# A mixture-of-experts kernel: the first layer's bias moves from TensorE to VectorE, two of eight weight splits from VectorE to GpSimd

## The chip, the cores and the metric

One core of one Trainium2 chip runs the program. The metric is the device time of one execution in microseconds (us); lower is better. The core has five engines that run their own instruction queues and meet at semaphores: TensorE (PE, matmuls; PEld is its weight load), VectorE (DVE), ScalarE (ACT), GpSimd (POOL) and SyncE (SP), which here only issues DMAs to 16 shared DMA engines.

## The reference

Three stages work on `x` of 8x64 tokens (512 rows) of width 512: a cross attention over `ctx_1024`, a self attention with given weights, and a mixture of experts. The change is in the third, whose whole computation is

```
gates = softmax(x @ Wg + bg);  top 2 of E=8 experts are kept and renormalised to g
h  = gelu(x @ W1[e] + b1[e])        # W1[e]: 512 x 2048, b1[e]: 2048
eo = h @ W2[e] + b2[e]              # W2[e]: 2048 x 512
x  = x + sum_e g[e] * eo[e]
```

## The kernel before

**Tiles.** Each token goes to two experts, so there are 1024 token rows. The kernel sorts them by expert into `sorted_x` in DRAM, each expert padded to whole tiles of 128 rows. With these inputs there are ten tiles: experts 0 and 1 have two each, experts 2 to 7 one each. I call them tile 0 to tile 9; expert e's last tile is its "change" tile, in which the weights of expert e+1 are brought in. `for_tiles` runs the same loops on every engine, with register bounds.

**Weights.** An expert's W1 and W2 are cut into eight units of 128x2048 fp32 (1 MB each), four of W1 and four of W2, in the order in which a tile uses them (`UNIT_ORDER`: W1 q0, q1, q2, W2 q0, W1 q3, W2 q1, q2, q3). SP loads a unit into one of four ring slots (`wu_raw`). ScalarE rounds it to `wu_hi` (`unit_hi`, L1454), VectorE makes the rest `wu_lo = wu_raw - wu_hi` (`unit_lo`, L1597), and that frees the slot: the load of unit v waits for `wu_lo` of the unit four places earlier (`load_next`, L1311). There is one set of eight `wu_hi`/`wu_lo` buffers, so `unit_hi(v)` for the next expert also waits until TensorE has used unit v of this one. All matmuls are done as three products (hi x hi, hi x lo, lo x hi), 12 of them for each quarter of a layer.

**A tile on TensorE**, in this order: `layer1(0)`, `layer1(1)`, `turn_hidden(0)`, `layer1(2)`, `turn_hidden(1)`, `layer2(0)`, `layer1(3)`, `turn_hidden(2)`, `layer2(1)`, `turn_hidden(3)`, `layer2(2)`, `turn_gathered(t + 1)`, `layer2(3)`. Each `layer1(q)` begins with one more matmul (L1678), ones x `b1rows`, which puts the bias into PSUM; `b1rows` holds the two halves (hi and lo) of the bias in rows 0 and 1 and zeros below. ScalarE's `gelu(q)` (L1460) reads the PSUM bank and writes `hid`; TensorE turns `hid`; `hidden_hi(q)` (ACT, L1466) and `hidden_lo(q)` (DVE, L1602) split it for `layer2(q)`. For the next tile `gathered_hi`/`gathered_lo` (L1440, L1579) split its turned tokens, and `layer1(0)` of the next tile waits for that (`g_lo`), for its weights and for the bias rows (`b1row_in`). At the end of a tile VectorE adds `b2row` and writes `eo` (L1620).

**The order on each engine is written by hand** and is in-order: whatever waits holds up what stands behind it. In a change tile VectorE does hidden_lo(0), unit_lo(0), unit_lo(1), hidden_lo(1), unit_lo(2), unit_lo(3), hidden_lo(2), unit_lo(4), hidden_lo(3), unit_lo(5), gathered_lo, eo, unit_lo(6), unit_lo(7). SP issues: tokens of the next tile (L1327, 256 KB), units 4 to 7 of expert e+1, then, after all four layer1 quarters, the bias rows of e+1 (L1320, 16 KB), units 0 to 3 of e+2, the store of `eo` (L1361, 256 KB) and `b2row` (L1323, one 2 KB row spread over 128 partitions, 256 KB).

**Before the first tile** the biases are split on chip: `b1_raw` is loaded, ScalarE and VectorE make its halves, SP writes them to DRAM (`b1_parts`) and GpSimd clears `b1rows`. Then VectorE makes unit_lo(4) to (7) of expert 0 (`first_lo`, L1499) ahead of its first tile's work. GpSimd scatters the sorted rows before the loop and fetches the results after it; during the tiles it has nothing to do.

Of the kernel before, what the change touches and what calls it, by code (L numbers as in the profile page):

```python
# [22 lines left out]

def perceiver_kernel(nc, x_in, ctx_in, Wq, bq, Wkv, bkv, Wproj, bproj,
# [38 lines left out]
    with ExitStack() as whole:  # L63
# [1149 lines left out]
        b1rows = sb(scope, "b1rows", [P, H], FR)  # L1213
        ones_r = sb(scope, "ones_r", [P, P], FR)
# [84 lines left out]
        with nc.Block() as block:  # L1299

            @block.sync
            def _(sp):
                sp.dma_start(Wg_raw[:, :, :], Wg.rearrange("(k p) e -> p k e", p=P)).then_inc(sem("wg_in"), 16)
                sp.dma_start(bgc[:, :], bg.rearrange("(e o) -> e o", o=1)).then_inc(sem("bg_in"), 16)
                sp.dma_start(b1_raw[:, :], b1.rearrange("e (c p) -> (e c) p", p=P)).then_inc(sem("b1_in"), 16)
# [26 lines left out]
                sp.wait_ge(sem("b1_split"), 1)  # L1332
                for part, b1_part in enumerate((b1_hi, b1_lo)):
                    sp.dma_start(b1_dram[part].rearrange("(r c) -> r c", c=P), f32(b1_part[:, :])) \
                        .then_inc(sem("b1_out"), 16)
                sp.wait_ge(sem("b1_out"), 32)
                sp.wait_ge(sem("b1rows_zeroed"), 1)
# [37 lines left out]
            def _(pool):  # L1375
                nc.gpsimd.memset(f32(b1rows[:, :]), 0.0).then_inc(sem("b1rows_zeroed"), 1)
# [113 lines left out]
            def _(dve):  # L1490
# [6 lines left out]
                def first_lo(v):  # L1497
                    dve.wait_ge(sem("wu_hi_done"), v + 1)
                    nc.vector.tensor_tensor(wu_lo(v), wu_raw[:, v % RING, :, :], f32(wu_hi[:, v, :, :]),  # L1499
                                            ALU.subtract).then_inc(sem("wu_lo_done"), 1)  # L1500

                dve.wait_ge(sem("b1_hi"), 1)
                nc.vector.tensor_tensor(b1_lo[:, :], b1_raw[:, :], f32(b1_hi[:, :]), ALU.subtract) \
                    .then_inc(sem("b1_split"), 1)
# [79 lines left out]
                dve.wait_ge(sem("b1_out"), 32)  # L1584
# [7 lines left out]
                def tile(e, t, change):  # L1592
                    def unit_lo(v):
                        if not change:
                            return
# [38 lines left out]
            def _(pe):  # L1634
# [120 lines left out]
```

## Time and profile before

| what | us |
|---|---|
| median of three runs (1578.81 to 1582.57) | 1578.88 |
| the profiled execution's own time | 1581.12 |
| its span | 1579.4 |
| mixture of experts, first to last tile (1294.5 to 1562.9 in the span) | 268.4 |
| TensorE busy | 1348.1 (85%) |
| VectorE busy | 956.2 (61%) |
| ScalarE busy | 756.9 (48%) |
| GpSimd busy | 45.5 (3%) |

Times inside the profile count from the start of the span. "Busy" of an engine says nothing of what it waited for; the DMA share is the mean over 16 engines of the time in which they had a packet under way, and can be near 1 at less than the highest rate. The profiled execution took 2.2 us longer than the median of the runs.

### The profile page before, as it was taken

The page shows a single profiled execution, that of the slowest core. Times are in us where ns is not written, and L with a number is a line of the kernel's source. Part 1 is how long each engine was busy: PE and PEld are TensorE (multiplying, and loading weights), DVE is VectorE, ACT ScalarE, POOL GpSimd, SP SyncE. Part 2 cuts the span into 40 slices and gives each one's busy share as a digit, 9 for nine tenths or more (in the row PEclk, how much of TensorE's full clock was granted, in tenths as well). Part 3 has the DMA queues.
Part 4 walks back from the last instruction along what each step waited for, and adds up shares of the span by engine and source line. Part 5 has one row for each costly group of instructions (what it writes and reads, how often), then busy time and mean ns, then how long its engine had stood idle before and what let it go on. Part 6 is the DMA issues. An engine that isn't in the chain of part 4 may idle for free. (4 is left out here: it accounts for less than half of the span.)

```text
span 1579.4 us, 21880 instructions
## 1 busy us (share of the span) xinstructions
PE 1348.1 (85%) x7363; PEld 1163.3 (74%) x7364; DVE 956.2 (61%) x1495; ACT 756.9 (48%) x1322; POOL 45.5 (3%) x50
## 2 busy tenths in 40 slices
PE   5999999999999999999999997306979529999995
PEld 4888888888888888888888886204758428777774
DVE  4666666666666666666666665345747564378782
ACT  3455555555555555455455554211222244387771
POOL 0000000000000000000000000021000030000001
PEclk8999999999999999999999999657979769999998
DMA  4210110110110110010110000275225264579993
GB/s 173 78 54 28 31 53 27 30 53 27 30 53 27 30 53 27 28 55 27 27 56 27 26 12 7 60 167 107 54 52 214 85 233 152 188 276 350 334 320 98
DMA packets 129458, 147.18 MB, mean 93 GB/s; under 512 B 66296, under 2 KB 66680, under 8 KB 129408
## 3 DMA queue, kind: packets, MB, share of 16 engines
q1 hardware_dynamic: 128144, 142.54, 28.9%
q0 software_dynamic: 1280, 4.20, 0.8%
q8 instruction: 20, 0.33, 0.1%
q14 instruction: 14, 0.11, 0.0%
HBM read 126.06 MB, written 20.64 MB: 93 GB/s over the span
## 5 line engine op out<-in xcount | busy, mean ns | idle before, releaser
L497 DVE SCALAR_TENSOR_TENSOR Ks<-ps_scores,bkc,Ks 64x384 fp32r<-64x384 f32 (+2 forms) x254 | 160.5, 632 | 205.2 <-ACT Ks L381 202.3
L459 ACT ACTIVATE Pr<-ps_scores,stat 128x705 f32<-128x705 f32 (+1 forms) x128 | 119.1, 931 | 324.3 <-DVE stat L590 324.3
L147 PE MATMUL ps_scores<-cT_hi,Wkv_hi 128*128 128x384 f32 (+2 forms) x508 | 179.7, 354 | 6.4 <-DVE Wkv_lo L519 6.4
L148 PE MATMUL ps_scores<-cT_lo,Wkv_hi 128*128 128x384 f32 (+2 forms) x508 | 176.0, 346 | 0.0
L149 PE MATMUL ps_scores<-cT_hi,Wkv_lo 128*128 128x384 f32 (+2 forms) x508 | 175.9, 346 | 0.0
L147 PE MATMUL ps_scores<-Wkv_hi,cT_hi 128*128 128x512 f32 (+1 forms) x412 | 168.5, 409 | 7.6 <-DVE Vs L503 7.1
L381 ACT ACTIVATE Ks<-ps_scores,bkc 64x384 fp32r<-64x384 f32 (+2 forms) x254 | 149.4, 588 | 35.5 <-PE ps_scores L149 33.8
L148 PE MATMUL ps_scores<-Wkv_lo,cT_hi 128*128 128x512 f32 (+1 forms) x412 | 162.8, 395 | 0.0
L149 PE MATMUL ps_scores<-Wkv_hi,cT_lo 128*128 128x512 f32 (+1 forms) x412 | 162.7, 395 | 0.0
L503 DVE TENSOR_TENSOR Vs<-ps_scores,Vs 128x512 fp32r<-128x512 f32 (+1 forms) x103 | 71.0, 689 | 133.5 <-ACT Vs L385 133.5
L747 PE MATMUL ps_turn<-ident,Pr 128*128 128x128 f32 x832 | 114.0, 275 | 30.8 <-ACT Pr L459 30.7
L575 DVE TENSOR_TENSOR PT<-ps_turn,PT 128x512 fp32r<-128x512 f32 (+2 forms) x256 | 129.7, 548 | 17.0 <-ACT PT L446 15.1
L1597 DVE TENSOR_TENSOR wu_lo<-wu_raw,wu_hi 128x2048 fp32r<-128x2048 f32 x56 | 126.6, 2286 | 15.0 <-ACT wu_hi L1454 14.6
L759 PE MATMUL ps_out<-PT,Vs 128*128 128x256 f32 x832 | 123.4, 286 | 14.0 <-DVE PT L579 9.5
L759 PEld LDWEIGHTS ps_out<-PT,Vs 128*128 128x128 f32 x832 | 113.8, 190 | 25.7 <-DVE PT L579 13.3
L590 DVE TENSOR_REDUCE stat<-ps_scores 128x1 f32<-128x705 f32 (+1 forms) x128 | 125.3, 979 | 3.4 <-DVE stats L606 3.4
L446 ACT CAST PT<-ps_turn 128x512 fp32r<-128x512 f32 (+2 forms) x256 | 110.6, 486 | 21.9 <-PE ps_turn L747 20.9
L747 PEld LDWEIGHTS ps_turn<-ident,Pr 128*128 128x128 f32 x832 | 92.5, 140 | 38.7 <-issue 27.5
L1454 ACT CAST wu_hi<-wu_raw 128x2048 fp32r<-128x2048 f32 x56 | 105.9, 1922 | 18.8 <-DMA wu_raw<-in_L_ffn_W_dram 17.8
L147 PEld LDWEIGHTS ps_scores<-cT_hi,Wkv_hi 128*128 128x128 f32 x508 | 96.4, 190 | 12.1 <-issue 6.8
L149 PEld LDWEIGHTS ps_scores<-cT_hi,Wkv_lo 128*128 128x128 f32 x508 | 96.0, 189 | 5.9
L148 PEld LDWEIGHTS ps_scores<-cT_lo,Wkv_hi 128*128 128x128 f32 x508 | 96.2, 189 | 5.2
(300 smaller groups left out, 2424.2 us busy)
## 6 DMA issues: line engine op xcount, KB each, us to landing
wu_raw<-in_L_ffn_W_dram SPq DMA_DIRECT2D x64, 1024.0 KB, 7.7
raw<-in_ctx_dram SPq DMA_DIRECT2D x16, 768.0 KB, 4.5
raw<-in_ctx_dram SPq DMA_DIRECT2D x8, 1024.0 KB, 5.2
raw<-in_ctx_dram SPq DMA_DIRECT2D x8, 512.0 KB
o_heads<-U SPq DMA_DIRECT2D x64, 64.0 KB, 1.8
oA<-o_heads SPq DMA_DIRECT2D x8, 512.0 KB, 15.8
sorted_x<-zeros SPq DMA_DIRECT2D x1, 4096.0 KB, 14.7
sorted_out<-zeros SPq DMA_DIRECT2D x1, 4096.0 KB, 24.4
```

The lines of the kernel that those rows point to most:

```text
L147: nc.tensor.matmul(out_ap, sh, mh, start=(i == 0), stop=False)
L148: nc.tensor.matmul(out_ap, sh, ml, start=False, stop=False)
L149: last = nc.tensor.matmul(out_ap, sl, mh, start=False, stop=(i == len(pairs) - 1))
L381: ins = nc.scalar.activation(Ks[c][0:64, 2 * i + h, o:o + wide], acc[64 * h:64 * h + 64, 0:wide], ACT.Identity, bias=bkc[:, 2 * i + h:2 * ...
L446: ins = nc.scalar.copy(PT[:, full[0]:full[-1] + 1, 0, :], acc[:, 0:P * len(full)].rearrange("p (t r) -> p t r", r=P))
L459: nc.scalar.activation(Pr[:, i % 2, 0:VALID[c]], S_cols(c, 0, VALID[c]), ACT.Exp, bias=stat[:, 0, c, i:i + 1], accum_out=stat[:, 1, c, i:i ...
L497: ins = nc.vector.scalar_tensor_tensor(out=Ks[c][64:128, j, o:o + wide], in0=acc[64 * h:64 * h + 64, 0:wide], scalar=bkc[:, j:j + 1], in1= ...
L575: ins = nc.vector.tensor_tensor(PT[:, full[0]:full[-1] + 1, 1, :], acc[:, 0:P * len(full)].rearrange("p (t r) -> p t r", r=P), f32(PT[:, f ...
L590: nc.vector.tensor_reduce(stat[:, 0, c, i:i + 1], S_cols(c, 0, VALID[c]), AX.X, ALU.max, negate=True).then_inc(sem("s_max"), 1)
L747: ins = nc.tensor.matmul(bank(P_BANKS[q])[0:M, at:at + P], Pr[:, (i - 1) % 2, t * P:t * P + M], ident[:, :], is_transpose=True, start=True ...
L759: ins = nc.tensor.matmul(psO_heads, Vs[c][0:M, t, i - 1, :], PT[0:M, t, :, :].rearrange("p a r -> p (a r)"), start=(t == 0), stop=(t == CH ...
L1597: nc.vector.tensor_tensor(wu_lo(v), wu_raw[:, v % RING, :, :], f32(wu_hi[:, v, :, :]), ALU.subtract).then_inc(sem("wu_lo_done"), 1)
```

## The change

VectorE adds the first layer's bias while it moves a PSUM bank to `hid`, from a `b1rows` that now holds the whole bias row of 2048 in all 128 partitions (one broadcast DMA of 8 KB to each partition, 1 MB, straight from `b1`). The four bias matmuls of a tile, the on-chip split of b1, its DRAM copy and TensorE's wait for `b1row_in` are gone; the wait is now in front of VectorE's `bias(0)`. ScalarE's gelu works on `hid` in place. GpSimd makes `wu_lo` of units 3 and 7; VectorE keeps six. Expert 0's eight units all stay on VectorE. The orders on ScalarE and VectorE are new.

```diff
-        b1rows = sb(scope, "b1rows", [P, H], FR)
-        ones_r = sb(scope, "ones_r", [P, P], FR)
+        b1rows = sb(scope, "b1rows", [P, H])
...
+        POOL_UNITS = (3, 7)
+        DVE_UNITS = tuple(v for v in range(UNITS) if v not in POOL_UNITS)
+        def lo_sem(v):
+            return sem("wu_lo_by_pool" if v in POOL_UNITS else "wu_lo_by_dve")
...
                 def load_next(e, v):
-                    sp.wait_ge(sem("wu_lo_done"), e * UNITS + v - RING + 1)
+                    sp.wait_ge(lo_sem((v + RING) % UNITS), lo_count(e if v >= RING else e - 1, (v + RING) % UNITS))
                 def load_b1(e):
-                    sp.dma_start(f32(b1rows[0:2, :]), b1_dram[:, bass.ds(e * H, H)]).then_inc(sem("b1row_in"), 16)
+                    sp.dma_start(b1rows[:, :], b1[bass.ds(e, 1), :].rearrange("a h -> (a h)").partition_broadcast(P)) \
+                        .then_inc(sem("b1row_in"), 16)
...
-                        sp.wait_ge(sem("l1_made"), t * QT + QT)
+                        sp.wait_ge(sem("h_biased"), t * QT + QT)
                         load_b1(e + 1)
...
+                def tile(e, t, change):          # GpSimd
+                    if change:
+                        for v in POOL_UNITS:
+                            pool.wait_ge(sem("wu_hi_done"), (e + 1) * UNITS + v + 1)
+                            nc.gpsimd.tensor_tensor(wu_lo(v), wu_raw[:, v % RING, :, :], f32(wu_hi[:, v, :, :]),
+                                                    ALU.subtract).then_inc(lo_sem(v), 1)
...
                     def gelu(q):                 # ScalarE
-                        act.wait_ge(sem("l1_made"), t * QT + q + 1)
-                        if q >= 2:
-                            act.wait_ge(sem("h_turned"), t * QT + q - 1)
-                        nc.scalar.activation(hid[:, q % 2, :], bank(q), ACT.Gelu).then_inc(sem("h_made"), 1)
+                        act.wait_ge(sem("h_biased"), t * QT + q + 1)
+                        nc.scalar.activation(hid[:, q % 2, :], hid[:, q % 2, :], ACT.Gelu).then_inc(sem("h_made"), 1)
                     gelu(0)
+                    unit_hi(0)
                     gelu(1)
                     hidden_hi(0)
-                    unit_hi(0)
                     unit_hi(1)
+                    hidden_hi(1)
                     gelu(2)
-                    hidden_hi(1)
                     unit_hi(2)
                     unit_hi(3)
+                    hidden_hi(2)
                     gelu(3)
-                    hidden_hi(2)
                     unit_hi(4)
...
+                    def bias(q):                 # VectorE
+                        dve.wait_ge(sem("l1_made"), t * QT + q + 1)
+                        if q == 0:
+                            dve.wait_ge(sem("b1row_in"), 16 * (e + 1))
+                        if q >= 2:
+                            dve.wait_ge(sem("h_turned"), t * QT + q - 1)
+                        nc.vector.tensor_tensor(hid[:, q % 2, :], bank(q), b1rows[:, q * 512:(q + 1) * 512], ALU.add) \
+                            .then_inc(sem("h_biased"), 1)
+                    bias(0)
+                    bias(1)
                     hidden_lo(0)
                     unit_lo(0)
+                    bias(2)
+                    hidden_lo(1)
                     unit_lo(1)
-                    hidden_lo(1)
                     unit_lo(2)
-                    unit_lo(3)
+                    bias(3)
                     hidden_lo(2)
                     unit_lo(4)
                     hidden_lo(3)
...
                     unit_lo(6)
-                    unit_lo(7)
...
                     def layer1(q):               # TensorE
-                        nc.tensor.matmul(bank(q), ones_r[:, :], b1rows[:, cols], start=True, stop=False)
...
-                    pe.wait_ge(sem("b1row_in"), 16 * (e + 1))
```

## Rows read from the trace of the kernel before

**Rows 1.** The page's first part: busy time, share and instructions of TensorE.

```profile
PE 1348.1 (85%) x7363; PEld 1163.3 (74%) x7364; DVE 956.2 (61%) x1495; ACT 756.9 (48%) x1322; POOL 45.5 (3%) x50
```

**Rows 2.** Windows of tiles 0 to 4, 8 and 9: length, busy, PEclk, DMA share, GB/s.

```profile
1294.48:1322.04 27.56, 27.56 (x121) 22.49 (x122) 12.26 (x9) 13.81 (x15) 0.00 (x0) 0.91 0.55 198
1322.04:1349.76 27.72, 25.52 (x122) 20.57 (x120) 19.14 (x14) 18.48 (x17) 0.00 (x0) 1.00 0.59 204
1349.76:1376.65 26.89, 26.89 (x121) 21.98 (x122) 6.66 (x7) 8.72 (x12) 0.00 (x0) 0.94 0.42 152
1376.65:1403.43 26.78, 25.51 (x121) 20.56 (x120) 18.07 (x14) 17.74 (x16) 0.00 (x0) 1.00 0.58 197
1403.43:1430.01 26.58, 25.63 (x121) 20.68 (x121) 21.54 (x14) 20.81 (x18) 0.00 (x0) 1.00 0.95 337
...
1510.19:1537.35 27.16, 25.77 (x121) 20.63 (x121) 22.40 (x16) 21.25 (x19) 0.00 (x0) 1.00 0.90 316
1537.35:1562.92 25.57, 25.43 (x120) 20.62 (x120) 7.81 (x7) 6.51 (x10) 3.84 (x4) 1.00 0.27 73
```

**Rows 3.** The chain that ended last, around tile 6's bias and its successor's start.

```profile
1459.59 0.23 PE ps_scores L1678
...
1475.84 6.94 DMA b1rows<-b_parts
1482.96 0.49 PE ps_scores L1678
```

**Rows 4.** VectorE's timeline in tile 6 (start, length, line, what, idle before).

```profile
1470.54 4.49 DVE L1597 TENSOR_TENSOR wu_lo<-wu_raw,wu_hi 128x2048 fp32r<-128x2048 f32 x2
...
1475.86 2.29 DVE L1597 TENSOR_TENSOR wu_lo<-wu_raw,wu_hi 128x2048 fp32r<-128x2048 f32 x1 [0.23 <-ACT wu_hi L1454]
...
1479.83 2.29 DVE L1597 TENSOR_TENSOR wu_lo<-wu_raw,wu_hi 128x2048 fp32r<-128x2048 f32 x1 [1.08 <-ACT wu_hi L1454]
1482.04 0.68 DVE L1579 TENSOR_TENSOR gT_lo<-ps_turn,gT_hi 128x512 fp32r<-128x512 f32 x1
```

**Rows 5.** ScalarE's timeline in tile 6: a gelu, and a unit that waited for its load.

```profile
1462.61 0.60 ACT L1460 ACTIVATE hid<-ps_scores 128x512 f32<-128x512 f32 x1 [2.07 <-PE ps_scores L1683]
...
1477.89 1.91 ACT L1454 CAST wu_hi<-wu_raw 128x2048 fp32r<-128x2048 f32 x1 [1.44 <-DMA wu_raw<-in_L_ffn_W_dram]
```

**Rows 6.** The DMA view of 1454 to 1462, a stretch with loads queued behind each other.

```profile
DMA packets 1549, 3.08 MB, mean 385 GB/s; under 512 B 50, under 2 KB 50, under 8 KB 1547
```

**Rows 7.** The first stage's end: GpSimd alone (L913), then GpSimd beside VectorE.

```profile
1048.72 4.94 POOL L913 TENSOR_TENSOR oA<-oA 128x512 f32<-128x512 f32 x4 [30.66 <-DMA oA<-o_heads]
...
L918 POOL TENSOR_TENSOR oA<-oA,oR x4: 1278/1496/1727, 1053.6 to 1057.7; 128x512 f32<-128x512 f32 x4
...
L994 DVE SCALAR_TENSOR_TENSOR oT<-oA,bvc x4: 740/1692/1749, 1055.0 to 1059.9; 128x512 f32<-128x512 f32 x4
```

**Rows 8.** DMA issues, KB and us to landing: 1537 to 1545, then 1034 to 1042.

```profile
sorted_out<-eo SPq DMA_DIRECT2D x1, 256.0 KB, 2.1
b2row<-in_L_ffn_b_dram SPq DMA_DIRECT2D x1, 256.0 KB, 4.0
...
x_sum<-in_x_dram SPq DMA_DIRECT2D x1, 1024.0 KB, 17.5
bpr<-in_L_xattn_bproj_dram SPq DMA_DIRECT2D x1, 256.0 KB, 13.3
```

**Rows 9.** SyncE's timeline, when the last two of these were issued.

```profile
1036.65 4.74 SPq L869 DMA_DIRECT2D x_sum<-in_x_dram  x1
1041.43 2.60 SPq L870 DMA_DIRECT2D bpr<-in_L_xattn_bproj_dram  x1
```

**Rows 10.** Tile 0: VectorE's last first splits, and TensorE's first turn of hidden.

```profile
1295.35 8.90 DVE L1499 TENSOR_TENSOR wu_lo<-wu_raw,wu_hi 128x2048 fp32r<-128x2048 f32 x4 [1.11 <-ACT wu_hi L1418]
...
1302.83 0.60 PE L1691 MATMUL ps_turn<-ident,hid 128*128 128x128 f32 x4
```

**Rows 11.** VectorE adds a row to a PSUM bank (eo), all ten tiles.

```profile
L1620 DVE TENSOR_TENSOR eo<-ps_out,b2row x10: 681/691/692, 1322.4 to 1562.9; 128x512 f32<-128x512 f32 x10
```

More of the change, by code:

```diff
@@ L1238, in perceiver_kernel @@
         lgT = sb(gating, "lgT", [NE, T])
-        b1_raw = sb(gating, "b1_raw", [P, P])
-        b1_hi = sb(gating, "b1_hi", [P, P], FR)
-        b1_lo = sb(gating, "b1_lo", [P, P], FR)
         before = sb(gating, "before", [P, P], BF16)
@@ L1272, in wu_lo, with lo_count @@
             return wu_lo_back[:, UNITS - 1 - v, :, :]
-        b1_dram = nc.dram_tensor("b1_parts", [2, NE * H], F32, kind="Internal").ap()
         EO_CREDIT = 16
+        POOL_UNITS = (3, 7)
+        DVE_UNITS = tuple(v for v in range(UNITS) if v not in POOL_UNITS)
+        def lo_sem(v):
+            return sem("wu_lo_by_pool" if v in POOL_UNITS else "wu_lo_by_dve")
+        def lo_count(e, v):
+            own = POOL_UNITS if v in POOL_UNITS else DVE_UNITS
+            return e * len(own) + own.index(v) + 1
         def load_tile(eng, tiles, e):
@@ L1304, in _ @@
                 sp.dma_start(bgc[:, :], bg.rearrange("(e o) -> e o", o=1)).then_inc(sem("bg_in"), 16)
-                sp.dma_start(b1_raw[:, :], b1.rearrange("e (c p) -> (e c) p", p=P)).then_inc(sem("b1_in"), 16)
                 def load_unit(e, v):
@@ L1331, in _ @@
                 load_b2(0)
[L1332 to L1337, printed above, removed]
                 load_b1(0)
@@ L1375, in _ @@
             def _(pool):
-                nc.gpsimd.memset(f32(b1rows[:, :]), 0.0).then_inc(sem("b1rows_zeroed"), 1)
                 nc.gpsimd.memset(before[:, :], 1.0).then_inc(sem("masks_set"), 1)
@@ L1401, in _ @@
                 pool.wait_ge(sem("table_ready"), 1)
+                def tile(e, t, change):
[4 more added lines that the diff above has]
+                                                    ALU.subtract).then_inc(lo_sem(v), 1)
+                for_tiles(pool, tile)
                 first = load_tile(pool, first_i, NE - 1)
-                pool.wait_ge(sem("wu_lo_done"), NE * UNITS)
+                for v in (UNITS - 2, UNITS - 1):
+                    pool.wait_ge(lo_sem(v), lo_count(NE - 1, v))
                 pool.wait_ge(sem("eo_stored"), first * 16 + EO_CREDIT)
@@ L1422, in _ @@
                 nc.scalar.copy(Wg_hi[:, :, :], Wg_raw[:, :, :]).then_inc(sem("wg_hi"), 1)
-                act.wait_ge(sem("b1_in"), 16)
-                nc.scalar.copy(b1_hi[:, :], b1_raw[:, :]).then_inc(sem("b1_hi"), 1)
-                nc.scalar.activation(ones_r[:, :], ident[:, :], ACT.Copy, bias=1.0, scale=0.0).then_inc(sem("ones_r"), 1)
                 turn_scalar(act, 3, x3T_hi)
@@ L1499, in first_lo @@
                     nc.vector.tensor_tensor(wu_lo(v), wu_raw[:, v % RING, :, :], f32(wu_hi[:, v, :, :]),
[L1500 to L1504, printed above, removed]
+                                            ALU.subtract).then_inc(lo_sem(v), 1)
                 step = [0]
@@ L1583, in _ @@
                 gathered_lo(0)
-                dve.wait_ge(sem("b1_out"), 32)
                 dve.wait_ge(sem("x_sorted"), 16 * 2 * TT)
@@ L1593, in unit_lo @@
                     def unit_lo(v):
+                        assert v in DVE_UNITS
                         if not change:
@@ L1597, in unit_lo @@
                         nc.vector.tensor_tensor(wu_lo(v), wu_raw[:, v % RING, :, :], f32(wu_hi[:, v, :, :]),
-                                                ALU.subtract).then_inc(sem("wu_lo_done"), 1)
+                                                ALU.subtract).then_inc(lo_sem(v), 1)
                     def hidden_lo(q):
@@ L1669, in _ @@
                 turn_gathered(0)
-                pe.wait_ge(sem("ones_r"), 1)
-                pe.wait_ge(sem("b1rows_zeroed"), 1)
                 def tile(e, t, change):
@@ L1675, in layer1 @@
                         v = UNIT_OF[("1", q)]
-                        pe.wait_ge(sem("wu_lo_done"), e * UNITS + v + 1)
-                        cols = slice(q * 512, (q + 1) * 512)
-                        nc.tensor.matmul(bank(q), ones_r[:, :], b1rows[:, cols], start=True, stop=False)
+                        pe.wait_ge(lo_sem(v), lo_count(e, v))
                         for k in range(KC):
                             wh, wl = wu_hi[:, v, k, :], wu_lo(v)[:, k, :]
-                            nc.tensor.matmul(bank(q), gT_hi[:, k, :], wh, start=False, stop=False)
+                            nc.tensor.matmul(bank(q), gT_hi[:, k, :], wh, start=(k == 0), stop=False)
                             nc.tensor.matmul(bank(q), gT_hi[:, k, :], wl, start=False, stop=False)
@@ L1697, in layer2 @@
                         v = UNIT_OF[("2", q)]
-                        pe.wait_ge(sem("wu_lo_done"), e * UNITS + v + 1)
+                        pe.wait_ge(lo_sem(v), lo_count(e, v))
                         pe.wait_ge(sem("h_lo"), t * QT + q + 1)
```

## The prediction

> **What bounds the kernel now.** I read the page's busy shares first: TensorE is busy 85% of the span [rows 1], which says where to look and no more. Then the windows, cut at the first matmul of each tile [rows 2]. The reader is to see two kinds of tile. In tiles 0 to 3 the DMA engines have a share of 0.42 to 0.59. From tile 4 on every tile is a change tile, eight weight units come in per tile, and the share is 0.90 to 1.00 at about 340 GB/s; TensorE is busy 25.6 of 26.6 us. So in tiles 4 to 7 both are nearly full. Then the chain of waits [rows 3]: it runs through the bias-row DMA, issued 1475.84 behind four units, landed 6.94 us later, and tile 7 starts on it. Last the timelines of tile 6. VectorE ends unit_lo(5) at 1482.1 and gathered_lo at 1482.7 [rows 4]; TensorE could have started 0.25 us later in any case, so taking away the bias wait alone brings next to nothing there. And unit_lo(5) was late because ScalarE stood 1.44 us for unit 5's load [rows 5]. The true loop is: load, unit_hi, unit_lo, slot free, load. How full can the queue run? With loads queued behind each other it moved 385 GB/s [rows 6].
>
> **The change, part by part.** I count from a tile's start, s = 0, with the offsets of tile 6 (start 1456.35, next start 1482.96).
>
> *Bias matmuls.* Four fewer per tile, 0.23 us each [rows 3], 0.92 us of TensorE. In tiles 2 and 9, where TensorE has no gap and nothing else is late (no weights are converted in them but for the first units' rest), that is on the path: -0.9 each. In change tiles it only moves TensorE's wait.
>
> *Bytes.* A single-tile expert moves 8 units of 1.049 MB, three transfers of 0.262 MB and 16 KB of bias, 9.19 MB. The bias row becomes 128 x 8 KB = 1.049 MB, so 10.22 MB, 11% more, on engines with a share near 1. At 385 GB/s [rows 6] that takes 26.5 us; at the 345 GB/s of 9.19 MB in tile 6's 26.61 us [rows 3] it takes 29.6 us. The first is the case in which longer queues fill every dip; the second the case in which the dips stay. The dips of today come from slots that are not yet free, and GpSimd will hold two slots longer (below), so I don't expect the full rate; but the bias transfer itself sits in the queue where a dip would be. I take the middle, 365 GB/s: 28.0 us per tile.
>
> *Does a broadcast row cost more than its bytes?* Two rows bound it [rows 8, 9]. bpr, one 2 KB row to 128 partitions, issued at 1041.43 behind x_sum, landed at 1054.7; x_sum at 1036.65 + 17.5 = 1054.2: 0.6 us for 256 KB, 440 GB/s, as good as any. b2row issued to an almost empty queue landed after 4.0 us where a store of the same size took 2.1. In tiles 4 to 7 the bias row is in a full queue like bpr, so I take its bytes alone and keep the other end as a rival.
>
> *GpSimd's two units.* GpSimd did four 128x512 tensor_tensor in 4.94 us by itself [rows 7], the same elements as one unit: 4.9 us against VectorE's 2.29 [rows 4]. Is it really beside VectorE? L994, a VectorE instruction that like unit_lo reads both inputs from SBUF, took 0.74 us when alone and 1.69 to 1.75 beside GpSimd's L918, which itself stretched from 1.28 to 1.73 [rows 7]. They took turns. So I count unit_lo on VectorE and a GpSimd unit as one after the other; bias, hidden_lo and gathered_lo read one input from PSUM and are not held. Bounds for this: no turns (L918's shortest, 1.28) and full turns.
>
> The Trainium skill says the same in "SBUF — State Buffer", section "Who interferes with whom": a VectorE instruction with two SBUF inputs contends with a GpSimd one that reads SBUF, and the first to start blocks the other for its whole length. By that rule, the trace agrees (1.75 against 0.74 us). "GPSIMD Engine Reference", section 3.1, has 4.50 us for a tensor_tensor of 2048 elements where the trace gives 4.94; the sum below would be 0.4 us per change tile lower by it.
>
> *The walk of a change tile.* layer1(0) and (1) are 24 matmuls, 5.5 us. bias(1) 0.69 [rows 11], gelu(1) 0.60 [rows 5], hidden_hi(0) about the same, hidden_lo(0) 0.7, with 0.1 between steps: 8.4. (unit_hi(0) on ScalarE now lies ahead of gelu(1), but starts at 4.4 after gelu(0), and is done at 6.4.) unit_lo(0) to 10.7, bias(2) 11.4, hidden_lo(1) 12.1, unit_lo(1) 14.3, unit_lo(2) 16.6. Before, unit_lo(2) ended at 16.4 (the first half of the pair at 1470.54) and unit_lo(3) at 18.7 [rows 4]. GpSimd now starts unit 3 at 16.6, ends at 21.5. bias(3) and hidden_lo(2) go beside it; unit_lo(4), which before ran at 19.5 to 21.8, waits to 21.5 and ends at 23.8; hidden_lo(3) 24.4; unit_lo(5) 26.7; gathered_lo 27.3; next tile at 27.5. layer2(3) starts at 24.5 and its 12 matmuls end at 27.3, so TensorE stands for a time equal to what it saved. Without turns unit_lo(4) keeps its time and the next tile could start at 26.2. So a change tile takes 27.5 by its engines; tiles 4 to 7 take the larger of that and the DMA's 28.0.
>
> *The bias wait moves to bias(0)*, at 3.0 of the next tile, three us later than TensorE's was. Behind it on VectorE stand bias(1) and everything else, on ScalarE gelu(0) and unit_hi(0). The row's issue moves from 19.5 to about 22 (it follows unit 7, which follows GpSimd's unit 3), and its landing from 26.4 to 22 + 2 (a small transfer's time to landing in an empty queue [rows 8]) + 2.7 (unit 7) + 2.7 = 29.4, against 28 + 3.0 = 31.0 when it is asked for. Covered by 1.6 us; gone if the row takes twice its bytes' time.
>
> *Tile 0.* VectorE makes unit_lo(4) to (7) until 1304.2 [rows 10]; nothing waited for it before. Now bias(0) stands behind: 1304.9, gelu(0) 1305.5, turn_hidden(0) 1305.6 instead of 1302.83 [rows 10], +2.8; layer1(2) and (3) give back 0.46: +2.3. The first two bias matmuls are saved into the wait.
>
> *Prologue.* The split, its DRAM round trip and GpSimd's memset ran beside the wait for the sorted rows: 0. Cover gone: none of them is on the path to the scatter either way.
>
> **The sum**, against the profiled execution (1581.1, of which 1579.4 is the span; 2.2 above the median): tile 0 +2.3; tile 1 27.5 for 27.72, -0.2; tile 2 -0.9; tile 3 27.5 for 26.78, +0.7; tiles 4 to 7 4 x 28.0 = 112.0 for 106.76 (1403.43 to 1510.19), +5.2; tile 8, which loads only four units, 27.5 for 27.16, +0.3; tile 9 -0.9. Together +6.5. On the median of 1578.9: 1585.
>
> **Rivals.**
>
> *A. The engines share the work and the queue fills (faster or equal).* Place: tiles 4 to 8. GpSimd and VectorE don't take turns, so VectorE is freed of two units, 4.6 us, for 2.8 us of bias; tiles 1, 3 and 8 take 26.2 (-1.5, -0.6, -1.0) and tiles 4 to 7 the DMA's 26.5 at 385 GB/s (-0.8 together). With tile 0's +2.3 and -1.8 of tiles 2 and 9: -3.4, 1575.5. It decides from the point where a change tile falls under 26.8. For it: full stretches of 385 do occur [rows 6], and unit_hi(0) is 2.7 us earlier. Against it: L994 beside L918 [rows 7], and 11% more bytes at a share of 0.99. The DMA floor keeps even this case within reach of no change.
>
> *B. The dips stay.* 345 GB/s, 29.6 us in tiles 4 to 7: 118.4 for 106.76, +11.6 in place of +5.2: 1591.5. For it: a slot under GpSimd is held 2.6 us longer, so fewer loads are under way; today's rate is that of a share of 0.99. Against it: the queue is asked for more.
>
> *C. The broadcast row is slow.* If each 256 KB costs 1.9 us more (4.0 against 2.1 [rows 8]), the 1 MB costs up to 7.6 us more; half of that, 3.8, on tiles 4 to 7 on top of 28.0, is 4 x 3.8 = 15 more: 1600, and up to 1615. bias(0) would be seen waiting for its DMA. Against it: bpr's 0.6 us [rows 8, 9].
>
> *D. The change doesn't do what it says*: GpSimd's units start late, since its loop bounds are read behind the scatter. The scatter ends before tile 0 and its first unit is needed in tile 1, so no.
>
> **How the numbers follow.** Forecast (turns taken, DMA rate between): 0.45, its own range 1580 to 1589. A 0.30, between 1571 and 1580. B 0.15. C 0.08. D and others 0.02. The range 1573 to 1597 leaves out A's best end, C and the rest, about 0.17. A measurement of this kernel can tell some 0.3%, 4.7 us. Below 1574.2: the better half of A, 0.15. Above 1583.6: two thirds of the forecast (0.30), B, C and the rest, 0.53. Between: 0.32.
>
> **What would show it.** Windows cut at layer1(0): tiles 4 to 7 at 27.5 to 28.5, with a higher GB/s than 345 and a share near 1; tile 2 and 9 shorter by 0.9; tile 0 longer by 2.3 with TensorE waiting at its first turn of hidden. GpSimd's unit at 4.9 us, longer when it starts inside a unit_lo, and unit_lo(4) at more than 2.29. In the chain unit_lo by GpSimd in place of the bias DMA. I am wrong if unit_lo stays at 2.29 while GpSimd runs (A), if the GB/s doesn't rise (B), or if bias(0) waits for its row in tiles 4 to 8 (C).

## The result, and the profile after

The changed kernel takes 1589.08 us (median of 13 runs, 1587.4 to 1592.06), the kernel before 1579.59 us beside it (13 runs): ratio 1.0057, 95% interval 1.0046 to 1.0067. The change costs 9.5 us; 1585 was forecast. The profiled execution took 1588.58 us with a span of 1586.8, 7.4 more than the span before; the ten tiles went from 268.44 to 274.86 us, +6.4. Of the rest of the 9.5, 1.0 lies outside the tiles (0.4 ahead of the first, 0.6 behind the last), and 2.0 is choice of execution: the profiled one of before lay 1.5 us over its median, that of after 0.5 under.

The page's first part, of the changed kernel, answers to [rows 1]:

```profile
PE 1344.1 (85%) x7323; PEld 1158.3 (73%) x7324; DVE 954.3 (60%) x1520; ACT 758.3 (48%) x1320; POOL 114.8 (7%) x64
```

TensorE does 4.0 us less, VectorE about as much as before (it lost two unit splits per expert change and got four bias adds per tile). The loss is in no engine's busy time: it is in waits. (40 matmuls of 0.23 us are gone, 9.2 us. TensorE's busy time in the ten tiles falls by 5.1 only, since it ran longer at the lower clock in tiles 0, 6 and 8 and shorter in tile 2.) The windows of the ten tiles, of the changed kernel, answer to [rows 2] (length; busy us of TensorE, its loads, VectorE, ScalarE, GpSimd; PEclk, DMA share, GB/s):

```profile
1294.89:1326.44 31.55, 28.41 (x116) 22.78 (x117) 14.94 (x13) 14.13 (x15) 0.00 (x0) 0.87 0.49 175
1326.44:1352.71 26.27, 24.47 (x117) 19.86 (x116) 18.70 (x15) 17.82 (x16) 5.13 (x1) 1.00 0.59 197
1352.71:1377.04 24.33, 24.33 (x118) 20.04 (x117) 9.11 (x11) 9.79 (x13) 4.62 (x1) 1.00 0.63 230
...
1403.31:1430.59 27.28, 24.70 (x118) 19.87 (x117) 19.57 (x16) 21.05 (x18) 10.56 (x2) 1.00 1.02 376
1430.59:1457.86 27.27, 24.82 (x117) 19.84 (x117) 19.58 (x16) 21.09 (x18) 10.54 (x2) 1.00 1.01 371
1457.86:1488.37 30.51, 26.99 (x117) 20.98 (x117) 19.65 (x16) 21.16 (x18) 9.41 (x2) 0.94 0.98 346
1488.37:1515.49 27.12, 24.89 (x118) 19.81 (x116) 20.72 (x16) 21.03 (x18) 10.55 (x2) 1.00 0.99 363
1515.49:1544.89 29.40, 26.47 (x117) 20.84 (x117) 20.31 (x16) 21.07 (x18) 9.74 (x2) 0.95 1.01 371
1544.89:1569.75 24.86, 24.72 (x117) 20.04 (x115) 9.12 (x11) 7.06 (x10) 9.26 (x5) 0.99 0.28 76
```

Tile 0 lost 4.0 us and tiles 4 to 8 together 7.7; tiles 1 to 3 gained 4.5 (tile 3 has tile 1's length) and tile 9 0.7. In tiles 4 to 8 the DMA share is 0.98 to 1.02 and the rate 346 to 376 GB/s, so more bytes pass and the queue is full. The same five tiles before, as one window:

```profile
1403.43:1537.35 133.92, 128.51 (x601) 103.45 (x601) 108.19 (x71) 104.96 (x91) 0.00 (x0) 1.00 0.97 339
```

The waits in the tiles (what waited, for what: us in total, times, longest), two lines of the kernel before, then the changed kernel from 1306.1 to the end of the last tile:

```profile
PE ps_scores L1678 <- DMA b1rows<-b_parts: 6.1, 5, 2.2
...
PE ps_out L1704 <- DVE h_lo L1602: 1.8, 2, 1.4
```

```profile
ACT wu_hi L1460 <- DMA wu_raw<-in_L_ffn_W_dram: 26.2, 27, 2.9
PE ps_out L1712 <- DVE h_lo L1603: 16.7, 9, 2.6
...
DVE hid L1612 <- DMA b1rows<-in_L_ffn_b_dram: 2.4, 3, 1.2
```

TensorE's wait for bias rows, 6.1 us in five places before, is gone. Instead it stands 16.7 us in nine places, the seven longer ones, 1.8 to 2.6 us each, ahead of layer2(3), for `hidden_lo(3)`, which on VectorE is behind `unit_lo(4)`. In tiles 4 to 8 that is behind unit 4's load, for which ScalarE's `unit_hi(4)` waited up to 1.5 us. In tiles 1 and 3, where the DMA share is 0.59, unit 4 was there in time; `unit_lo(4)` took 3.5 us because GpSimd's unit 3 was under way (VectorE, then GpSimd, in tile 1):

```profile
1345.59 3.54 DVE L1598 TENSOR_TENSOR wu_lo<-wu_raw,wu_hi 128x2048 fp32r<-128x2048 f32 x1 [1.90 <-ACT wu_hi L1460]
...
1341.86 5.13 POOL L1406 TENSOR_TENSOR wu_lo<-wu_raw,wu_hi 128x2048 fp32r<-128x2048 f32 x1 [54.10 <-ACT wu_hi L1460]
```

What a stop can do beyond its own length is seen in tile 6, TensorE's timeline:

```profile
1480.98 0.60 PE L1676 MATMUL ps_turn<-ident,xg 128*128 128x128 f32 x4
1483.96 0.65 PE L1712 MATMUL ps_out<-wu_hi,h_hi 128*128 128x512 f32 x1 [2.38 <-DVE h_lo L1603]
1484.41 0.63 PE L1713 MATMUL ps_out<-wu_lo,h_hi 128*128 128x512 f32 x1
1484.83 0.63 PE L1714 MATMUL ps_out<-wu_hi,h_lo 128*128 128x512 f32 x1
...
1488.60 0.39 PE L1690 MATMUL ps_scores<-wu_lo,gT_hi 128*128 128x512 f32 x1
1488.83 0.39 PE L1691 MATMUL ps_scores<-wu_hi,gT_lo 128*128 128x512 f32 x1
```

After the 2.38 us stop the matmuls start 0.43 us apart instead of 0.23, the clock's lower level. Three windows of the same kernel, behind tile 6's stop, tile 8's and tile 0's, give the price:

```profile
1484.00:1488.40 4.40, 4.40 (x13) 3.45 (x14) 2.62 (x2) 2.01 (x2) 0.00 (x0) 0.61 1.05 351
...
1540.00:1545.00 5.00, 4.21 (x13) 3.38 (x14) 3.44 (x4) 2.10 (x2) 0.00 (x0) 0.71 1.02 404
...
1306.10:1311.00 4.90, 4.90 (x17) 3.90 (x18) 0.69 (x1) 1.10 (x2) 0.00 (x0) 0.65 1.06 384
```

4.40 x 0.39 is 1.7 us in tile 6, 5.00 x 0.29 is 1.5 us in tile 8, 4.90 x 0.35 is 1.7 us in tile 0, each on top of the stop. In tile 8 the fall came some 1.4 us after TensorE had started again. It doesn't follow every stop: those of tiles 4, 5 and 7 (2.58, 2.41 and 2.22 us) left the clock at 1.00.

GpSimd's and VectorE's `wu_lo` by duration (min/median/max in ns), 1400 to 1545, and one meeting of the two in tile 7:

```profile
L1598 DVE TENSOR_TENSOR wu_lo<-wu_raw,wu_hi x31: 2274/2281/3454, 1400.3 to 1540.6; 128x2048 fp32r<-128x2048 f32 x31
L1406 POOL TENSOR_TENSOR wu_lo<-wu_raw,wu_hi x10: 4616/5122/5437, 1405.6 to 1532.8; 128x2048 fp32r<-128x2048 f32 x10
...
1504.63 5.12 POOL L1406 TENSOR_TENSOR wu_lo<-wu_raw,wu_hi 128x2048 fp32r<-128x2048 f32 x1 [8.58 <-ACT wu_hi L1460]
...
1508.45 3.45 DVE L1598 TENSOR_TENSOR wu_lo<-wu_raw,wu_hi 128x2048 fp32r<-128x2048 f32 x1 [1.98 <-ACT wu_hi L1460]
```

GpSimd's ends at 1509.75; VectorE's, begun at 1508.45, ends 2.15 us after that. That is nearly the whole 2.28 us of a unit: VectorE's did next to nothing until GpSimd's was done. They take turns.

The chain of waits of the changed kernel, 1400 to 1545, answers to [rows 3]; GpSimd's `wu_lo` has 14.3% of it, where before there was the bias DMA:

```profile
1490.62 5.44 POOL wu_lo L1406
1496.07 0.37 SPq L1316
...
1500.44 6.04 DMA wu_raw<-in_L_ffn_W_dram
1506.50 1.93 ACT wu_hi L1460
1508.45 3.46 DVE wu_lo L1598
```

GpSimd's unit 7 holds SP up in `load_next`. Behind it SP stores `eo`, fetches `b2row`, reads the next tile's loop bounds, fetches its tokens and only then, 4.4 us after GpSimd's end, issues unit 4, which tile 7's stop waits for.

### The profile page after: what moved, and what is told of

It is laid out like the page before. It is cut to its first block and busy times, and to the rows that moved or that the text cites. A ratio compares the mean times of both kernels' runs of the same rounds, so it can differ in the third digit from the quotient of the medians.

```text
span 1586.8 us, 21932 instructions
## 1 busy us (share of the span) xinstructions
PE 1344.1 (85%) x7323; PEld 1158.3 (73%) x7324; DVE 954.3 (60%) x1520; ACT 758.3 (48%) x1320; POOL 114.8 (7%) x64
## 5 line engine op out<-in xcount | busy, mean ns | idle before, releaser
L747 PE MATMUL ps_turn<-ident,Pr 128*128 128x128 f32 x832 | 114.8, 276 | 30.8 <-ACT Pr L459 30.6
L1460 ACT CAST wu_hi<-wu_raw 128x2048 fp32r<-128x2048 f32 x56 | 106.2, 1906 | 30.2 <-DMA wu_raw<-in_L_ffn_W_dram 26.2
L1598 DVE TENSOR_TENSOR wu_lo<-wu_raw,wu_hi 128x2048 fp32r<-128x2048 f32 x42 | 99.6, 2386 | 18.4 <-ACT wu_hi L1460 18.4
```

The source lines that it names most:

```text
L747: ins = nc.tensor.matmul(bank(P_BANKS[q])[0:M, at:at + P], Pr[:, (i - 1) % 2, t * P:t * P + M], ident[:, :], is_transpose=True, start=True ...
L1460: nc.scalar.copy(wu_hi[:, v, :, :], wu_raw[:, v % RING, :, :]).then_inc(sem("wu_hi_done"), 1)
```

## The experiments

Ratios are to the kernel before, run beside them. "t4-8" is the length of tiles 4 to 8 in the one profiled execution (before: 133.9; changed: 141.6), tile 0 likewise (27.56; 31.55). There is one profile to a kernel, and it can lie some us off its median: a and j have the same code from tile 1 on, and their tiles 4 to 8 took 134.3 and 139.5. So where the two differ the ratio decides. By the intervals two ratios must be about 0.002 apart to be told from each other.

| label | ratio, 95% interval | median us | tile 0 | t4-8 |
|---|---|---|---|---|
| a_small | 1.0040 [1.0021, 1.0059] | 1584.28 | 31.54 | 134.3 |
| b_alldve | 1.0049 [1.0034, 1.0065] | 1586.48 | 31.54 | 139.3 |
| c_poolonly | 1.0022 [1.0006, 1.0039] | 1584.85 | 27.49 | 136.7 |
| d_firstpool | 1.0029 [1.0015, 1.0042] | 1584.36 | 27.76 | 140.3 |
| e_before_early | 0.9978 [0.9968, 0.9989] | 1576.96 | 27.55 | 134.7 |
| g_after_order | 1.0035 [1.0016, 1.0054] | 1586.23 | 31.57 | 141.6 |
| h_before_order | 0.9961 [0.9947, 0.9975] | 1573.92 | 28.02 | 130.6 |
| j_small_firstpool | 1.0019 [1.0003, 1.0035] | 1581.89 | 27.78 | 139.5 |
| k_small_dve | 1.0043 [1.0027, 1.0060] | 1586.60 | 31.55 | 140.2 |
| l_small_first_order | 0.9955 [0.9938, 0.9972] | 1574.40 | 27.77 | 135.3 |
| m_best_pool | 0.9966 [0.9951, 0.9980] | 1574.94 | 27.53 | 131.6 |
| n_first_order | 1.0014 [1.0000, 1.0029] | 1583.57 | 27.78 | 141.7 |

**The bytes: a_small.** The changed kernel with a bias row of 16 KB; it leaves out the biases of experts 1 to 7 in all partitions but two, so it is a measuring device and not a complete kernel. j, k and l share this.

```diff
-                        load_b1(e + 1)
+                        load_b1_rows(e + 1, 2)      # partition_broadcast(2) into b1rows[0:2, :]
```

> The changed kernel, but from expert 1 on the bias load writes only partitions 0 and 1 (16 KB instead of 1 MB per expert; the other 126 partitions keep expert 0's bias row, so the biases of experts 1 to 7 are left out there). Theory 1 (the added bytes fill the DMA queue, and the tiles are as long as their bytes take at about 365 GB/s): tiles 4 to 7, 28.05 us each in the changed kernel, fall to 9.19 MB / 0.365 = 25.2 us and then meet the engines' own length, so 26.3 to 26.8; tile 8 (29.40) loses its stall and its half-clock stretch and falls to about 27; in all 7 to 9 us less than the changed kernel, a ratio to the kernel before of 1.000. Theory 2 (GpSimd holds the two ring slots too long and the bytes only fill waits that are there anyway): tiles 4 to 7 stay at 27.3 or more, ratio 1.004 to 1.006.

Its profile gave back 7.3 us of the 7.7 in tiles 4 to 8, but that was its fastest run (1581.24); by the ratios 0.0017 came back, 2.7 us, and the two intervals overlap. The profile's 7.3 us are theory 1's, the ratio is theory 2's. Stops ahead of layer2(3) of 1.8 to 2.9 us stayed in seven tiles. So the bytes alone are not the loss.

**GpSimd's share: b_alldve** (the changed kernel, all low halves on VectorE) and **c_poolonly** (the kernel before, units 3 and 7 on GpSimd).

```diff
-        POOL_UNITS = (3, 7)
+        POOL_UNITS = ()
...
                     hidden_lo(2)
+                    unit_lo(3)
                     unit_lo(4)
...
                     unit_lo(6)
+                    unit_lo(7)
```

> The changed kernel with all eight low halves back on VectorE (unit 3 after hidden_lo(2), unit 7 last); the 1 MB bias row and bias on VectorE stay. Theory 1 (bytes): tiles 4 to 7 stay at 27.7 to 28.5, ratio to the kernel before 1.004 to 1.007. Theory 2 (GpSimd's 4.6 to 5.4 us in place of 2.3 holds the slots): units 3' and 4 are issued 2 to 3 us earlier, TensorE's 2.2 to 2.6 us stop before layer2(3) goes, tiles 4 to 7 at 27.0 or less, ratio 1.002 or less.

```diff
+        POOL_UNITS = (3, 7)          # and GpSimd's tile loop, as in the change
...
                     unit_lo(2)
-                    unit_lo(3)
                     hidden_lo(2)
...
                     unit_lo(6)
-                    unit_lo(7)
```

> The kernel before with only the second half of the change: GpSimd makes the low halves of units 3 and 7, bias products and 16 KB bias rows and both old orders kept. Theory 1 (bytes): no byte is added, tiles 4 to 7 within 0.3 us of 26.7, ratio 0.999 to 1.001. Theory 2 (slots held by GpSimd): the bias row's issue behind unit 7 moves 2 us later and TensorE waits for it, tiles 4 to 7 at 28 or more, ratio 1.004 or more.

Taking GpSimd out of the changed kernel makes no difference that can be told (1.0049, 1.0057), as theory 1 had it: the stops ahead of layer2(3) shrink to 0.75 to 1.18 us, but new ones of 0.97 to 2.03 come at the first turn of hidden, since `bias(0)` is now behind `unit_lo(7)`. Putting GpSimd into the kernel before costs 0.0022, between the two theories, and not by the bias row's wait that theory 2 named: TensorE's wait for it falls to 1.5 us, and its waits for `hidden_lo(3)` ahead of layer2(3) grow from 1.8 to 9.1 us, in seven tiles.

**Tile 0: d_firstpool.** Expert 0's units 3 and 7 go to GpSimd, ahead of its tile loop.

```diff
+                for v in POOL_UNITS:                 # GpSimd
+                    pool.wait_ge(sem("wu_hi_done"), v + 1)
+                    nc.gpsimd.tensor_tensor(wu_lo(v), wu_raw[:, v % RING, :, :], f32(wu_hi[:, v, :, :]),
+                                            ALU.subtract).then_inc(lo_sem(v), 1)
...
-                first_lo(3)                          # VectorE
...
-                for v in range(RING, UNITS):
+                for v in range(RING, UNITS - 1):
                     first_lo(v)
```

> The changed kernel, with expert 0's units 3 and 7 also made by GpSimd, so that VectorE's bias(0) of tile 0 stands behind three first splits and not four. In the changed kernel tile 0 took 31.55 us (27.56 before), TensorE stopped 3.1 us at the first turn of hidden and then ran at half clock for some us. If that stop is VectorE's four first splits: the stop shrinks to about 1 us, tile 0 falls to 28.5 to 30, and the ratio to the kernel before is 0.001 to 0.002 lower than the changed kernel's 1.0057. If it is ScalarE (its four first casts and a table load ahead of gelu(0)): no change.

TensorE's stop at tile 0's first turn goes from 3.14 to 0.71 us and tile 0 from 31.55 to 27.76. The ratio falls by 0.0028, 4.4 us, more than the 0.001 to 0.002 expected: tile 0's loss is shown, and it is the first splits on VectorE.

**The wait by itself: e_before_early.** The kernel before, its 16 KB bias load issued ahead of unit 7 instead of behind it.

```diff
-                        for v in range(RING, UNITS):
+                        for v in range(RING, UNITS - 1):
                             load_next(e + 1, v)
                         sp.wait_ge(sem("l1_made"), t * QT + QT)
                         load_b1(e + 1)
+                        load_next(e + 1, UNITS - 1)
```

> The kernel before; SP only issues the next expert's 16 KB bias load ahead of unit 7 and not behind it. In the kernel before TensorE waited 6.1 us in 5 places for that load (2.20 us in front of tile 2, 1.27 in front of tile 4). If removing TensorE's wait were the useful half of the change: tile 1 falls from 27.72 to 25.5 to 26, tile 3 from 26.78 to about 26, tiles 4 to 7 by no more than 0.3 each (VectorE's gathered_lo ends 0.25 us before), together 3 to 5 us, ratio to the kernel before 0.997 to 0.999. If the wait was only the visible one of several: ratio 1.000.

0.9978, as expected, and TensorE no longer waits for bias rows anywhere: one moved line takes away the wait that the change was paying for with 1 MB.

**The order: g_after_order and h_before_order.** The split of hidden(3) goes ahead of unit 4's, that of the gathered tokens ahead of unit 5's, on ScalarE and VectorE alike; g in the changed kernel, h in the one of e.

```diff
                     hidden_lo(2)
-                    unit_lo(4)
                     hidden_lo(3)
-                    unit_lo(5)
+                    unit_lo(4)
                     gathered_lo(t + 1)
+                    unit_lo(5)
```

> The changed kernel with hidden_hi(3)/hidden_lo(3) ahead of unit 4's split and gathered_hi/gathered_lo ahead of unit 5's, on both engines. Theory 1 (bytes bound tiles 4 to 7, and TensorE's stop of 2.2 to 2.6 us before layer2(3) is where they show): the stop before layer2(3) goes, but tiles 4 to 7 keep 27.5 to 28.2 us because the next stop takes its place; only tiles 1 and 3 (1.8 us stop at a DMA share of 0.59) get shorter, by 1 to 1.8 each, to about 24.6 to 25.2; ratio to the kernel before 1.002 to 1.004. Theory 2 (the order behind unit 4's load is the bound): tiles 4 to 8 fall to 26 or less, ratio 0.998 to 1.000.

> The kernel before with both moves: the bias load ahead of unit 7, and the splits of hidden(3) and of the gathered tokens ahead of those of units 4 and 5. If TensorE (25.1 us of work per tile) and 9.19 MB at 365 GB/s (25.2 us) are the bounds: change tiles at 25.2 to 26, the ten tiles together 260 to 264 us (268.4 before), ratio 0.995 to 0.998, faster than both kernels. If the ring of four slots bounds (load, unit_hi, unit_lo): tiles 4 to 7 stay at 26.4 or more and only tiles 1 and 3 gain, ratio 0.998 to 1.000.

In g (theory 1, by ratio and tiles) the stops ahead of layer2(3) are gone, and from tile 4 on others of 1.5 to 2.8 us stand at the first turn: `bias(0)` waits 6.8 us in five places for the 1 MB row. In h the same edit brings the lowest ratio of a complete kernel here, 0.9961. The edit moves two splits at once; which of them does it was not tested. h's windows of tiles 4, 5 and 8:

```profile
1403.55:1429.97 26.42, 25.48 (x122) 20.68 (x121) 21.76 (x15) 20.85 (x19) 0.00 (x0) 1.00 0.98 350
1429.97:1455.99 26.02, 25.42 (x122) 20.75 (x121) 21.79 (x15) 20.71 (x19) 0.00 (x0) 1.00 1.00 354
...
1508.75:1534.12 25.37, 25.37 (x121) 20.76 (x120) 21.67 (x15) 20.74 (x19) 0.00 (x0) 1.00 0.98 356
```

TensorE is busy for all of tile 8. (The columns are those of the windows above. The profile is of h's slowest run, 1577.75.)

**Two repairs at once: j_small_firstpool.** a and d together.

> The changed kernel with both suspected costs taken away: the bias load of experts 1 to 7 writes only partitions 0 and 1 (their biases are left out in the other rows), and GpSimd makes expert 0's units 3 and 7. If the 1 MB bias rows and VectorE's place in tile 0 are the whole loss: tile 0 27.8, tiles 4 to 8 134 us together, the ten tiles 263 to 264 us, ratio to the kernel before 0.997 to 0.999. If something outside the tiles or in the other edits costs too: ratio 1.000 or more.

A miss: 1.0019, where less than 1 was expected. Without bytes and without tile 0's stop, TensorE still stood here, in tile 4:

```profile
1425.09 0.47 PE L1720 MATMUL ps_out<-wu_hi,h_hi 128*128 128x512 f32 x1 [3.51 <-DVE h_lo L1611]
```

The theory that the bytes make this stop falls with it. What is left is the order, `hidden_lo(3)` behind a unit that isn't there yet, and g, in which that order is changed and the stop is gone with all the bytes in place, shows it.

**Neither bytes nor GpSimd: k_small_dve.** a and b together.

> The changed kernel, bias row of 16 KB for experts 1 to 7 (partitions 0 and 1 alone are written, so their biases are left out in the other partitions) and all eight low halves on VectorE: neither the bytes nor GpSimd. What is left of the change is tile 0 (+3.9 us) and VectorE's four biases, against 0.92 us per tile less TensorE. Theory 1 (the loss in tiles 4 to 8 is the bytes plus GpSimd's late slots): tiles 4 to 8 come to 132 to 135 us as before (133.9), ratio 1.000 to 1.002. Rival (VectorE itself cannot hold 2.8 us more in a change tile, so unit_lo(7) ahead of the next bias(0) makes TensorE stop at its first turn, as in the kernel with all low halves on VectorE and the 1 MB row): tiles 4 to 8 stay above 137 us, ratio 1.003 or more.

The rival had it: 1.0043. TensorE stops up to 2.1 us at its first turns, here in tile 6, and tile 5's window has 28.2 us at 320 GB/s, less than h moves in 26.0:

```profile
1464.70 0.56 PE L1697 MATMUL ps_turn<-ident,hid 128*128 128x128 f32 x3 [1.84 <-ACT hid L1460]
...
1428.97:1457.14 28.17, 24.96 (x117) 19.78 (x117) 24.00 (x18) 20.95 (x18) 0.00 (x0) 1.00 0.96 320
```

VectorE has 24.0 us of work in such a tile, and TensorE waits for it at both ends of its order.

**All three, and each put back: l_small_first_order** (a, d and g's order), **n_first_order** (l with the 1 MB row) and **m_best_pool** (h with GpSimd's units).

> The changed kernel without its three suspected losses: the 16 KB bias row (experts 1 to 7; their biases left out beyond partitions 0 and 1), expert 0's units 3 and 7 on GpSimd, and hidden(3) split ahead of unit 4, the gathered tokens ahead of unit 5. Theory 1 (bytes, tile 0 and the stop before layer2(3) make up the whole loss, and the bias matmuls are a gain once they are gone): tiles 4 to 8 at 26 us or less each, ten tiles at 258 to 262 us, ratio 0.995 to 0.997. Rival (GpSimd's 4.6 to 5.4 us hold the slots and the loop stays at the DMA's dips whatever the order): tiles 4 to 8 stay at 27 us or more, ratio 0.999 or more.

> The changed kernel with the 1 MB bias row of every expert, expert 0's units 3 and 7 on GpSimd, and the splits of hidden(3) and of the gathered tokens moved forward: the same as the kernel that measured 0.9955, but for the 7.2 MB of bias bytes. Theory 1 (the bytes are the largest part of the loss: the queue has no room for them): tiles 4 to 7 at 28 us each as in the changed kernel, ten tiles 8 us or more longer than with the small row, ratio 1.001 to 1.003. Rival (the bytes only hurt through the late GpSimd slots and the stop before layer2(3), both gone here): ratio within 0.002 of the small row's, 0.9955 to 0.9975.

> The kernel before with the 16 KB bias load ahead of unit 7 and the two splits moved forward (0.996), and with units 3 and 7 on GpSimd in addition. Theory 1 (GpSimd's 4.6 us unit delays a slot and thereby a load, and VectorE was not short of time): slower than the same kernel with all eight on VectorE, ratio 0.997 to 1.000, GpSimd's unit 7 in the chain of waits. Rival (GpSimd only hurt through the old order, in which hidden_lo(3) stood behind unit 4): same or better, 0.994 to 0.996.

l measured 0.9955, as theory 1 has it, though its tiles 4 to 8 took 26.1 to 27.9 us where it had 26 or less; at 135.3 they are no shorter than before (133.9). What l gains on the kernel before lies in tiles 1 to 3, 73.6 us for 81.4. n measured 1.0014, as its theory 1 has it. They differ in the bias bytes alone; windows of tiles 5 and 7, first l, then n:

```profile
1421.70:1447.78 26.08, 24.78 (x116) 19.94 (x117) 19.57 (x17) 20.99 (x18) 9.71 (x2) 1.00 0.98 344
...
1475.72:1502.50 26.78, 24.82 (x117) 19.65 (x116) 19.66 (x17) 20.79 (x18) 10.84 (x2) 1.00 0.93 325
```

```profile
1425.09:1453.47 28.38, 26.15 (x118) 20.94 (x116) 19.79 (x17) 21.34 (x19) 9.69 (x2) 0.94 1.01 362
...
1481.86:1510.23 28.37, 25.10 (x117) 19.76 (x116) 19.65 (x17) 21.09 (x18) 9.71 (x2) 1.00 1.00 361
...
DVE hid L1616 <- DMA b1rows<-in_L_ffn_b_dram: 7.9, 6, 1.6
```

n's tiles 5 to 8 are all within 0.02 us of 28.38: a loop held by the queue, with `bias(0)` waiting for the row in each. m measured 0.9966, between its two theories and not to be told from h: under the new order no gain or loss by GpSimd's units can be seen.

**What follows together.** d, j, n and l have the same tile 0 and form a square:

| ratio | old order | new order |
|---|---|---|
| 1 MB row | 1.0029 (d) | 1.0014 (n) |
| 16 KB row | 1.0019 (j) | 0.9955 (l) |

The bytes cost 0.0010 in the old order and 0.0059 (9.3 us) in the new; the order is worth 0.0015 with the bytes and 0.0064 (10.1 us) without. The two small steps are within the noise, the two large ones are not, and the large ones exceed the small by 0.0049, give or take 0.003 by the intervals. In tiles 4 to 8 bytes and order are two limits, one behind the other: taking one away shows the other. In tiles 1 to 3, where the queue has room, the order brings 3.3 us with either bias row (76.9 to 73.6 us in the profiles). Tile 0 is a loss of its own, 0.0028 (after to d) or 0.0021 (g to n, within the noise). GpSimd's units cost 0.0022 in the old order of the kernel before; in the new one a cost would be under 0.003.

Do the four saved matmuls bring anything? In tiles 1 and 3, yes. Here is tile 1 of l, with the adds on VectorE, and of m, with the bias matmuls, both in the new order with GpSimd's units:

```profile
1321.02:1345.26 24.24, 24.24 (x117) 19.99 (x116) 15.48 (x15) 16.31 (x16) 5.15 (x1) 1.00 0.53 179
```

```profile
1323.26:1348.45 25.19, 25.19 (x122) 20.74 (x120) 13.09 (x11) 15.89 (x16) 5.34 (x1) 1.00 0.54 180
```

TensorE is busy throughout in both, and the tile is 0.95 us shorter, the price of four matmuls; n, with the 1 MB row, has 24.24 too. In tiles 4 to 8 nothing of it is left (l 135.3, m 131.6), and l and m as a whole differ by 0.0011 with intervals that overlap; l is not a complete kernel. No complete kernel with the bias on VectorE was faster than before.

## Why the prediction was nearly right

The direction and the range held, and the sum over the ten tiles was +6.5 forecast, +6.4 measured. That it fits so well is luck: tiles 0 and 8 were 3.6 us too low in the sum and tiles 1, 2 and 3 4.1 us too high, and these cancel. 1589.08 itself lies just past the forecast's own range of 1580 to 1589.

The main step, that tiles 4 to 7 take the larger of 27.5 us by the engines and 28.0 us by the bytes, is borne out to within a us a tile (27.1 to 27.3 where the clock held, 28.4 in n). It also says that the bytes alone are worth only 0.5 us a tile, 2 us in all, which is what a_small found (2.7).

- *Tiles 4 to 7*: 112.0 forecast, 112.18 measured (1403.31 to 1515.49). Their DMA mean, with tile 8, was 365 GB/s, the value taken:

```profile
DMA packets 24069, 51.68 MB, mean 365 GB/s; under 512 B 961, under 2 KB 961, under 8 KB 23361
...
b1rows<-in_L_ffn_b_dram SPq DMA_DIRECT2D x5, 1024.0 KB, 8.8
```

The sum is right, but the tiles are not 28.0 each: they are 27.1 to 27.3, and one 30.5 where the clock fell (1.7) and two short stops (0.39 and 0.63) came on top. Without these the four tiles would have come out some 3 us under the 112.0. n's even 28.4 is the picture that the prediction drew.
- *Tile 8*: +0.3 forecast, +2.2 measured. The step "tile 8, which loads only four units" was wrong: at 371 GB/s for 29.4 us it moved 10.9 MB, since the last expert's units 0 to 3, which stand in SP's order for tile 7, were still coming in. [rows 2] had it: 316 GB/s for 27.16 us is 8.6 MB before. 28.0 like its neighbours would have been +0.8; the lower clock after its 2.2 us stop (1.5) makes up about the other 1.4.
- *Tile 0*: the first turn came at s + 11.2, as worked out (8.4 before, + 2.8). Forecast +2.3, measured +4.0: the 1.7 us are those of the lower clock level after the stop. The step priced a stop at its length; d shows the whole term.
- *Tiles 2 and 9*: -0.9 each forecast, -2.6 and -0.7 measured. Tile 2's extra gain is the clock again: its PEclk was 0.94 before [rows 2], behind a bias wait, and is 1.00 now.
- *The walk of a change tile*: 27.5 forecast, 26.27 in tiles 1 and 3, 1.2 us too long in each. The steps are there in order, each a little earlier (forecast in brackets): unit_lo(2) ends at s + 16.0 (16.6), GpSimd's unit at 20.6 (21.5), unit_lo(4) at 22.7 (23.8). GpSimd began its unit at s + 15.4, inside unit_lo(2), and not behind it at 16.6; its unit then took 5.13 us (4.94 was taken [rows 7]; 4.62 when alone). That 26.27 is also rival A's value without turns, 26.2, is chance: the 3.54 us of unit_lo(4) are a turn.
- *Turns*: right. A VectorE `unit_lo` of 3.45 us beside GpSimd's, against 2.28, and GpSimd's 5.12 behind a running one. The section "Who interferes with whom" of the Trainium skill's "SBUF — State Buffer", cited in the prediction, is borne out by these; the 4.50 us of "GPSIMD Engine Reference", section 3.1, is nearer to the 4.62 than the 4.94 that stood in the sum. But in tiles 4 to 6 unit_lo(4) was not held up: unit 4 came so late that GpSimd was done.
- *The broadcast row*: costs its bytes only, as taken; rival C is out (n: 28.4 us per tile, not 31.8). Its issue came at s + 22.0 in tile 4, as forecast, its landing 8.8 later at the median (a weight unit of the same size took 7.4), about s + 30.8 instead of 29.4, so the cover of 1.6 us was used up: 2.4 us of waiting in three places (7.9 in six in n). This is the sign that the prediction named for C, but at C's price the tiles would be 3.8 us longer.
- *What was not seen*: that `hidden_lo(3)` behind unit 4 is what TensorE waits for. The walk had the stop (layer2(3) at 24.5), but not that moving `hidden_lo(3)` and the gathered tokens is worth 10 us once the bytes are gone, and that the old wait for the bias row could be had for a moved load.
- *Rival A* failed: the engines took turns, and with a share of 1 in every one of tiles 4 to 8 the queue gave 365 GB/s and not its 385. *B* would have had 29.6 us tiles at 345 GB/s; the rate did rise.

The medians moved 9.5 and the sum had 6.5; of the 3.0 between, 2.0 is the choice of profiled executions and 1.0 lies outside the tiles in the two spans. The cause of that last 1.0 is open.

## What to carry to other kernels

Where two resources are both nearly full, taking work off one by putting bytes on the other buys nothing; look first whether the wait can go by moving its small load forward in the queue, and whether a short step that the bound engine needs stands behind a long one that waits for a load. Test repairs together as well as singly: here each of three alone brought 0.2 to 0.3% (two of them no more than the noise), and together 1%. Price a stop of TensorE at more than its length: three of the eight long ones in the changed kernel cost 1.5 to 1.7 us more.

## What was not expected of the hardware

- After a stop of 3.14 us (tile 0) and of 2.38 and 2.21 us (tiles 6 and 8) the clock was granted at its lower level (1.2 GHz of 2.4) for part of the next 4 to 5 us, 1.5 to 1.7 us lost in each; after stops of 2.58, 2.41, 2.22 and twice 1.80 us it was not. What decides it, these traces don't show. So equal tiles of one kernel take 27.3 or 30.5 us. That the executions of one kernel differ by which tiles the clock strikes would follow, but was not traced.
- With the row of 1 MB the queue gave 365 GB/s over five tiles at a share of 1, and 359 in n; the 385 of [rows 6] is reached in slices, and did not last.
